# Weight-tile loads moved from SyncE's queue to GpSimd's, and a third buffer for the token blocks

## The chip, the cores and the metric

The kernel runs on all 8 cores of one Trainium2 chip, two cores to a batch element: both compute k and v of all its 4096 tokens, and each the rest for its own 2048 tokens. There is no exchange between cores. The metric is the device time in microseconds of the slowest core.

## The reference

One transformer layer on x of shape (4, 4096, 2048), with sandwich norms:

```python
x = x + layernorm(attn(layernorm(x), Wqkv, Wout))        # 16 heads of 128, RoPE, causal softmax
x = x + layernorm(ffn(layernorm(x), w1, w3, w2))         # hidden size 5461
# ffn: every weight is first made ternary
s = mean(abs(w));  wq = clip(round(w / s), -1, 1) * s
ffn(x) = (silu(x @ w1q.T) * (x @ w3q.T)) @ w2q.T
```

Each of w1, w3 and w2 therefore has to be read twice: once for mean(abs(w)), once to be made ternary.

## The kernel before

The program is written out by hand for five engines, with semaphores. `b.w(engine, sem, value)` is a wait that stands at that place in that engine's instruction stream; `b.dma(queue, ...)` issues a transfer at that place in the stream of SyncE (SP), ScalarE (ACT) or GpSimd (POOL). An engine that waits issues nothing that stands behind the wait. Five phases are divided by barriers.

**Phase 1, projections.** Three parts (q with 16 blocks, k with 32, v with 32) run over blocks of 128 tokens. The 16 MB of float32 weights of a part are loaded as bf16 by eight GpSimd DMAs (`wqkvT`), which wait for TensorE's last instruction of the part before. For block `tb`, `p1_loads(tb+1)` puts the load of the next block (`xin`, 1 MB, two buffers) and its cos and sin rows (`ctile`, `stile`, two buffers) on SP. TensorE makes two halves `dh` of 32 matmuls each (L372, L376). After the first half, `p1_stage_ln(tb+1)` normalizes the next block: VectorE (DVE) sums it (L258), ACT squares it (L260), small operations follow, DVE writes the result (L288), and TensorE transposes it (L299). For q and k, DVE applies RoPE (L390 to L400) to each half, TensorE transposes (L420), DVE copies (L428), and ACT issues four stores. For v, ACT evacuates each half (L407) and issues one store.

At the end of each block comes `emit_spass_tiles(2)`: two tiles of w1, w3 or w2 (139 in all, so they last for the first 70 of the 80 blocks) are loaded on SP into `wtl` (two buffers), ACT takes the absolute sum (L218), and GpSimd adds it to a running sum (L224 for a matrix's first tile, else L228). Before tile k is loaded, SP waits for ACT's sum of tile k-2. GpSimd waits for ACT's sum of tile k before it adds it. Of w1 and w3 every third tile has 1365 columns (682.5 KB), the others have 2048 (1 MB).

**Phase 2, attention.** There are 64 passes: four query slots with 8, 16, 24 and 32 key tiles, and 16 heads in each. In pass p, SP first issues the windows of pass p+2 (q, k and v of that head, `issue_windows`), once TensorE has ended pass p-1. TensorE makes scores (L589), ACT the exponentials (L601), DVE masks the last 8 key tiles (L611), TensorE multiplies with v and with ones (L627, L631); a short tail of the pass before (reciprocal L654, L660, L666, L671) is placed after the second pair. Then comes `emit_quant(3)`: three weight tiles (139 in all, so 46 passes have three and the 47th has one) are loaded on SP into `qtl` (two buffers), DVE makes them ternary in two operations (L523, L528), and ACT issues the store. SP waits for DVE's second operation on tile k-2 before it loads tile k; DVE waits for the load of k and for the store of k-2 (`rstg`, two buffers). As the third tile of a pass uses the buffers of the first, its load is issued when the first is done.

Phases 3 to 5 (output projection, w1 and w3, w2) aren't touched.

Of the kernel before, what the change touches and what calls it, by code (L numbers as in the profile page):

```python
# [48 lines left out]
def bcast_mid(ap2d, rep):  # L49
    return dataclasses.replace(ap2d, ap=[ap2d.ap[0], [0, rep], ap2d.ap[1]])  # L50
# [43 lines left out]
class Bld:  # L94
# [41 lines left out]
    def barrier(self, state):  # L136
        for sem in ["ld", "st"] + [f"d{i}" for i in range(8)] + [f"s{i}" for i in range(4)]:
            self.w("sync", sem, self.cnt[sem])
        for sem in ["sd", "act"] + [f"s{i}" for i in range(4)]:
            self.w("scalar", sem, self.cnt[sem])  # L140
        self.w("gpsimd", "gd", self.cnt["gd"])
        self.w("gpsimd", "gq", self.cnt["gq"])
        self.w("vector", "dve", self.cnt["dve"])
        self.w("tensor", "pe", self.cnt["pe"])
        for e in ENGS:
            inst = self.engobj.nop() if self.eng == e else None
            self.sig(inst, "ph", 1)
        tgt = self.cnt["ph"]
        self.engobj.wait_ge(self.sems["ph"], tgt)
# [3 lines left out]
def emit_program(b, t):  # L153
# [11 lines left out]
    i = b.V.memset(t["ones_f"][:], 1.0)  # L165
# [8 lines left out]
    fa = Carve(FAA, t["FA_COLS"])  # L174
    wsb = bf.take(16 * 2048)
    xnb = [bf.take(2048), bf.take(2048)]
# [2 lines left out]
    qks = [bf.take(1024), bf.take(1024)]  # L179
    fmstg = [bf.take(2048), bf.take(2048)]  # L180
    vstg = [bf.take(2048), bf.take(2048)]
    xin = [fa.take(2048), fa.take(2048)]
    ctile = [fa.take(128), fa.take(128)]
    stile = [fa.take(128), fa.take(128)]
    t1f = [fa.take(1024), fa.take(1024)]
    t2f = [fa.take(1024), fa.take(1024)]
    wtl = [fa.take(2048), fa.take(2048)]
# [14 lines left out]
    sp_done = {}  # L202
    sp_add = {}

    def emit_spass_tiles(n):
        for _ in range(n):
            if sp_idx[0] >= len(sp_tiles):
                return
            k = sp_idx[0]
            mat, r0, f0, fw, acc = sp_tiles[k]  # L210
            rows = 128 if mat != "w2T" else min(128, HID - r0)
            slot = k % 2
            b.w("sync", "act", sp_done.get(k - 2, 0))
            c_ld = b.dma("sync", f"d{4 + slot}", wtl[slot][0:rows, 0:fw],
                         t[mat][r0:r0 + rows, f0:f0 + fw])
            b.w("scalar", f"d{4 + slot}", c_ld)
            b.w("scalar", "gq", sp_add.get(k - 1, 0))
            i = b.A.activation(spscr[0:rows, 0:fw], wtl[slot][0:rows, 0:fw],  # L218
                               AF.Abs, accum_out=stats[0:rows, 28:29])
            c = b.sig(i, "act")  # L220
            sp_done[k] = c
            b.w("gpsimd", "act", c)
            if not acc_init[acc]:
                i = b.G.tensor_scalar(stats[0:rows, acc:acc + 1],  # L224
                                      stats[0:rows, 28:29], 1.0, None, ALU.mult)
                acc_init[acc] = True
            else:
                i = b.G.tensor_add(stats[0:rows, acc:acc + 1],  # L228
                                   stats[0:rows, acc:acc + 1],
                                   stats[0:rows, 28:29])  # L230
            c = b.sig(i, "gq")
            b.w("gpsimd", "gq", c)
            sp_add[k] = c
            sp_idx[0] += 1
# [8 lines left out]
    rope_done = {}  # L243
# [2 lines left out]
    fmstg_free = {}  # L246
    vstg_free = {}
    xin_free = {}
    mm_done = {}
    xnb_cons = {}  # L250
    xhT_mm = {}
# [59 lines left out]
    for pidx, (part, poff, nblk) in enumerate(parts):  # L311
# [13 lines left out]
        cnorm_map = {}  # L325

        def p1_loads(tb):
            par = tb % 2
            dcnt, acnt = xin_free.get(par, (0, 0))
            b.w("sync", "dve", dcnt)  # L330
            b.w("sync", "act", acnt)
            xld_map[tb] = b.dma("sync", f"d{par}", xin[par][:],
                                xsrc_t[tb * 128:(tb + 1) * 128, :])
            if part in ("q", "k"):
                b.w("sync", "dve", rope_done.get((par, 0), 0))
                b.w("sync", "dve", rope_done.get((par, 1), 0))
                b.dma("sync", f"d{2 + par}", ctile[par][:],
                      cos_d[tb * 128:(tb + 1) * 128, :])
                ccs_map[par] = b.dma("sync", f"d{2 + par}", stile[par][:],
                                     sin_d[tb * 128:(tb + 1) * 128, :])  # L340

        def p1_stage_ln(tb):
            par = tb % 2
            b.w("vector", f"d{par}", xld_map[tb])
            b.w("scalar", f"d{par}", xld_map[tb])
            b.w("vector", "pe", xnb_cons.get(par, 0))
            cnorm = ln_normalize(xin[par][:], xnb[par][:], tb)
            xin_free[par] = (cnorm, b.cnt["act"])
            cnorm_map[tb] = cnorm

        def p1_stage_tp(tb):
# [3 lines left out]
            xnb_cons[par] = b.cnt["pe"]  # L355

        p1_loads(0)
        p1_stage_ln(0)
        p1_stage_tp(0)
        for tb in range(nblk):  # L360
            par = tb % 2
            if tb + 1 < nblk:
                p1_loads(tb + 1)
            c_cs = ccs_map.get(par, 0)
            for dh in range(2):
                b.w("tensor", "act", vevac_done.get((dh,), 0))
                b.w("tensor", "dve", rope_done.get(("t1", dh), 0))
                b.w("tensor", "gd", wld)
                b.w("tensor", "dve", xhT_done[par])
                last = None  # L370
                for ec in range(16):
                    i = b.T.matmul(pa[:, dh * 1024: dh * 1024 + 512],  # L372
                                   xhT[par][:, ec * 128:(ec + 1) * 128],
                                   wsb3[:, ec, dh * 1024: dh * 1024 + 512],
                                   start=(ec == 0), stop=(ec == 15))
                    i2 = b.T.matmul(pa[:, dh * 1024 + 512: dh * 1024 + 1024],  # L376
                                    xhT[par][:, ec * 128:(ec + 1) * 128],
                                    wsb3[:, ec, dh * 1024 + 512: dh * 1024 + 1024],
                                    start=(ec == 0), stop=(ec == 15))
                    last = i2 if i2 is not None else i  # L380
                c_mm = b.sig(last, "pe")
                mm_done[(par, dh)] = c_mm
                paH = pa[:, dh * 1024:(dh + 1) * 1024]
                if part in ("q", "k"):
                    b.w("vector", "pe", c_mm)
                    b.w("vector", f"d{2 + par}", c_cs)
                    pa3 = _r(paH, "p (h d) -> p h d", h=8)
                    t13 = _r(t1f[dh][:], "p (h d) -> p h d", h=8)
                    cosb = bcast_mid(ctile[par][:], 8)
                    i = b.V.tensor_tensor(t13, pa3, cosb, ALU.mult)  # L390
                    b.sig(i, "dve")
                    for hf in range(2):
                        ov = half_view(t2f[dh][:], 8, hf)
                        iv = half_view(paH, 8, 1 - hf)
                        sv = half_bcast(stile[par][:], 8, hf)
                        i = b.V.tensor_tensor(ov, iv, sv, ALU.mult)
                        b.sig(i, "dve")
                    b.w("vector", "dve", b.cnt["dve"])
                    b.w("vector", "pe", qks_free.get(dh, 0))
                    i = b.V.tensor_add(qks[dh][:], t1f[dh][:], t2f[dh][:])  # L400
                    c = b.sig(i, "dve")
                    rope_done[("t1", dh)] = c
                    rope_done[(par, dh)] = c
                else:
                    b.w("scalar", "pe", c_mm)
                    b.w("scalar", f"s{2 + par}", vstg_free.get(par, 0))
                    i = b.A.activation(vstg[par][:, dh * 1024:(dh + 1) * 1024],  # L407
                                       paH, AF.Copy)
                    vevac_done[(dh,)] = b.sig(i, "act")
                if dh == 0 and tb + 1 < nblk:  # L410
                    p1_stage_ln(tb + 1)
# [98 lines left out]
    def emit_quant(n):  # L510
        for _ in range(n):
            k = q_idx[0]
            if k >= len(q_tiles):
                return
            mat, rsp, thb, r0, rows, f0, fw = q_tiles[k]
            slot = k % 2
            b.w("sync", "dve", q_v.get(k - 2, 0))
            c_ld = b.dma("sync", f"d{2 + slot}", qtl[slot][0:rows, 0:fw],
                         t[mat][r0:r0 + rows, f0:f0 + fw])
            q_ld[k] = c_ld  # L520
            b.w("vector", f"d{2 + slot}", c_ld)
            b.w("vector", f"s{2 + slot}", q_store.get(k - 2, 0))
            i = b.V.tensor_scalar(sqscr2[slot][0:rows, 0:fw],  # L523
                                  qtl[slot][0:rows, 0:fw],
# [543 lines left out]
def build_program():  # L1068
# [33 lines left out]
    with ExitStack() as ctx:  # L1102
# [10 lines left out]
        t["pa"] = En(nc.psum_tensor("pa", [128, 2048], F32))  # L1113
        t["pb"] = En(nc.psum_tensor("pb", [128, 2048], F32))
        sem_names = (["ld", "gd", "sd", "st", "pe", "dve", "act", "gq", "ph"]
                     + [f"d{i}" for i in range(8)] + [f"s{i}" for i in range(4)])
        sems = {n: En(nc.semaphore(n)) for n in sem_names}
        for val, idx in t["consts"].items():
            nc.const_aps.register(F32, val, t["cpool"][:, idx:idx + 1])
# [116 lines left out]
```

How the kernel before makes its waits and increments, by code:

```python
    def sig(self, inst, sem, n=1):  # L117
        self.cnt[sem] += n
        if inst is not None:
            inst.then_inc(self.sems[sem], n)
        return self.cnt[sem]
# [1 line left out]
    def w(self, eng, sem, val):  # L123
        if val <= 0:
            return
        assert val <= self.cnt[sem], (sem, val, self.cnt[sem])
        if self.eng == eng:
            self.engobj.wait_ge(self.sems[sem], val)
# [7 lines left out]
    def barrier(self, state):  # L136
        for sem in ["ld", "st"] + [f"d{i}" for i in range(8)] + [f"s{i}" for i in range(4)]:
            self.w("sync", sem, self.cnt[sem])
        for sem in ["sd", "act"] + [f"s{i}" for i in range(4)]:
            self.w("scalar", sem, self.cnt[sem])
        self.w("gpsimd", "gd", self.cnt["gd"])
        self.w("gpsimd", "gq", self.cnt["gq"])
        self.w("vector", "dve", self.cnt["dve"])
        self.w("tensor", "pe", self.cnt["pe"])
        for e in ENGS:
            inst = self.engobj.nop() if self.eng == e else None
            self.sig(inst, "ph", 1)
        tgt = self.cnt["ph"]
        self.engobj.wait_ge(self.sems["ph"], tgt)
```

## Time and profile before

| | us |
|---|---|
| median of 2 runs | 7228.25 (6972.67 and 7483.83) |
| the profiled execution | 6924.68 |
| its slowest core, core 3, first to last instruction | 6923.1 |
| the other cores | 6892.8 to 6922.9 |

In the profile of the slowest core TensorE is busy for 70% of the span, DVE for 33%, ACT for 20% and GpSimd for 1%. The chain of work that ended last is 60% TensorE and 17% DVE, and 7% DMA. Busy time is an average over phases that have different limits, so the phases are read one by one. In the rows of idle time, an engine's wait is put down to what ended last before it went on. A DMA's time to landing counts from the start of its issue.

### The profile page before, as it was taken

To read this page: it belongs to the slowest core of one execution; us is meant where nothing else is said; L and a number is where in the kernel's file an instruction comes from. 1 tells how busy PE (TensorE), PEld (TensorE's weight loads), DVE (VectorE), ACT (ScalarE), POOL (GpSimd) and SP (SyncE) were. 2 spreads that over 40 slices of the span, in tenths; PEclk is the share of its full clock that TensorE was granted. 3 is DMA by queue.
4 is the path that set the end of the run, shared out by engine and by line. 5 is a ranking of instruction groups with operands and counts; after the bars stand their busy time and mean duration, and the time that the engine had idled before them with its cause. 6 is when DMAs were issued, how large, how long until landed. Compare 5 with 4: busy or idle time off the path is not lost.

```text
span 6923.1 us, 58985 instructions; the slowest of 8 cores (6892.8 to 6923.1 us)
## 1 busy us (share of the span) xinstructions
PE 4868.7 (70%) x20684; PEld 1976.7 (29%) x20684; DVE 2250.4 (33%) x2417; ACT 1417.6 (20%) x1543; POOL 56.5 (1%) x175
## 2 busy tenths in 40 slices
PE   4775777759964455566579983444999999786666
PEld 2332333324420011111112221222444444332233
DVE  3543555523336655544432222332000000011122
ACT  1221222225411122233345540111000000000000
POOL 0000000000000000000000000000000000000000
PEclk8777888879986677677789986777999999898888
DMA  6446444376445545544533224323222222345544
GB/s 143 125 140 132 130 143 144 125 182 229 168 136 181 196 163 169 181 155 155 170 119 80 69 45 107 91 89 100 64 56 55 55 64 55 101 135 170 172 148 148
DMA packets 763499, 881.28 MB, mean 127 GB/s; under 512 B 538368, under 2 KB 629972, under 8 KB 715302
## 3 DMA queue, kind: packets, MB, share of 16 engines
q1 hardware_dynamic: 552540, 678.95, 31.6%
q10 hardware_dynamic: 177396, 165.01, 7.0%
q0 software_dynamic: 33280, 33.56, 3.4%
q8 instruction: 177, 2.90, 0.2%
q14 instruction: 106, 0.87, 0.1%
HBM read 729.18 MB, written 181.75 MB: 132 GB/s over the span
## 4 chain that ended last, share of the span: by engine, by line
PE 60%; DVE 17%; DMA 7%; issue 7%; ACT 5%; another core or an unknown queue 2%; SPq 1%; ACTq 1%; DVEq 0%; POOL 0%; POOLq 0%
PE pa L882 9%; PE pb L899 9%; PE pa L372 7%; PE pa L376 6%; PE pb L631 5%; PE pb L627 5%; PE pa L985 4%; PE pb L985 4%; PE pa L589 4%; ACT BFA L601 3%; DVE BFA L528 3%; PE pa L749 2%; PE pb L749 2%; PE pb L660 2%; DVE FAA L390 2%
## 5 line engine op out<-in xcount | busy, mean ns | idle before, releaser
L372 PE MATMUL pa<-BFA 128*128 128x512 bf16 x2560 | 1036.9, 405 | 252.1 <-DMA BFA<-wqkvT 174.0
L627 PE MATMUL pb<-BFA 128*128 128x512 bf16 x1280 | 546.7, 427 | 711.9 <-ACT BFA L601 459.8
L376 PE MATMUL pa<-BFA 128*128 128x512 bf16 x2560 | 1033.4, 404 | 0.0
L601 ACT ACTIVATE BFA<-pa,biascsb 128x1024 bf16<-128x1024 f32 x640 | 705.3, 1113 | 1437.6 <-DVE BFA L528 683.2
L882 PE MATMUL pa<-BFA 128*128 128x512 bf16 (+1 forms) x2752 | 603.2, 380 | 37.3 <-DMA BFA<-r3sp 37.3
L899 PE MATMUL pb<-BFA 128*128 128x512 bf16 (+1 forms) x2752 | 601.0, 379 | 0.0
L985 PE MATMUL pa<-BFA 128*128 128x512 bf16 (+1 forms) x1376 | 363.7, 388 | 256.5 <-DMA BFA<-w2rsp 235.9
L631 PE MATMUL pb<-BFA,ones_b 128*1 128x512 bf16 x1280 | 531.3, 415 | 0.0
L909 DVE SCALAR_TENSOR_TENSOR BFA<-pb,stats,BFA 128x2048 bf16<-128x2048 f32 (+1 forms) x43 | 101.1, 2351 | 1128.7 <-PE pb L899 1128.7
L611 DVE TENSOR_TENSOR BFA<-BFA 128x512 bf16<-128x512 bf16 x512 | 195.1, 422 | 834.7 <-ACT BFA L601 834.6
L627 PEld LDWEIGHTS pb<-BFA 128*128 128x128 bf16 x1280 | 127.3, 99 | 1088.3 <-issue 1082.5
L372 PEld LDWEIGHTS pa<-BFA 128*128 128x128 bf16 x2560 | 263.5, 103 | 604.1 <-issue 364.5
L589 PE MATMUL pa<-BFA 128*128 128x512 bf16 x1280 | 420.7, 422 | 20.1 <-DMA BFA<-vsp 20.1
L882 PEld LDWEIGHTS pa<-BFA 128*128 128x128 bf16 (+1 forms) x2752 | 270.7, 98 | 362.7 <-issue 40.5
L899 PEld LDWEIGHTS pb<-BFA 128*128 128x128 bf16 (+1 forms) x2752 | 271.1, 98 | 322.9
L985 PE MATMUL pb<-BFA 128*128 128x512 bf16 (+1 forms) x1376 | 360.3, 385 | 0.0
L376 PEld LDWEIGHTS pa<-BFA 128*128 128x128 bf16 x2560 | 262.4, 102 | 332.2 <-issue 90.3
L218 ACT ACTIVATE BFA<-FAA 128x2048 bf16<-128x2048 f32 (+1 forms) x139 | 247.3, 1779 | 533.1 <-DVE BFA L306 436.3
L528 DVE SCALAR_TENSOR_TENSOR BFA<-FAA,stats 128x2048 bf16<-128x2048 f32 (+1 forms) x139 | 304.2, 2189 | 14.9 <-DVE FAA L523 0.5
L890 ACT ACTIVATE BFA<-pa,stats 128x2048 bf16<-128x2048 f32 (+1 forms) x43 | 84.6, 1967 | 1076.5 <-PE pa L882 1076.5
L390 DVE TENSOR_TENSOR FAA<-pa,FAA 128x1024 f32<-128x1024 f32 x96 | 117.2, 1221 | 572.7 <-PE pa L376 572.7
L420 PE MATMUL pb<-identsb,BFA 128*128 128x128 bf16 x768 | 78.7, 264 | 266.0 <-DVE BFA L400 266.0
(83 smaller groups left out, 3357.0 us busy)
## 6 DMA issues: line engine op xcount, KB each, us to landing
FAA<-w2T SPq DMA_DIRECT2D x84, 1024.0 KB, 7.1
BFA<-w2rsp SPq DMA_DIRECT2D x336, 256.0 KB, 2.8
FAA<-w1T SPq DMA_DIRECT2D x64, 1024.0 KB, 9.0
FAA<-x_tok SPq DMA_DIRECT2D x64, 1024.0 KB, 8.7
FAA<-w3T SPq DMA_DIRECT2D x64, 1024.0 KB, 9.8
BFA<-vsp SPq DMA_DIRECT2D x160, 256.0 KB, 8.0
FAA<-x_own SPq DMA_DIRECT2D x32, 1024.0 KB, 9.0
BFA<-wqkvT POOLq DMA_DIRECT2D x24, 1024.0 KB, 38.4
```

The lines of the kernel that those rows point to most:

```text
L372: i = b.T.matmul(pa[:, dh * 1024: dh * 1024 + 512], xhT[par][:, ec * 128:(ec + 1) * 128], wsb3[:, ec, dh * 1024: dh * 1024 + 512], start=( ...
L376: i2 = b.T.matmul(pa[:, dh * 1024 + 512: dh * 1024 + 1024], xhT[par][:, ec * 128:(ec + 1) * 128], wsb3[:, ec, dh * 1024 + 512: dh * 1024 + ...
L390: i = b.V.tensor_tensor(t13, pa3, cosb, ALU.mult)
L528: i = b.V.scalar_tensor_tensor(rstg[slot][0:rows, 0:fw], qtl[slot][0:rows, 0:fw], stats[0:rows, thb + 1:thb + 2], sqscr2[slot][0:rows, 0:f ...
L589: i = b.T.matmul(pa[:, (2 * pr + kt % 2) * 512:(2 * pr + kt % 2 + 1) * 512], kwin[ring][:, kt * 128:(kt + 1) * 128], qwin[ring][:], start= ...
L601: i = b.A.activation(ptv, pa[:, pr * 1024:(pr + 1) * 1024], AF.Exp, bias=bc2, scale=SCL)
L627: i = b.T.matmul(ovb, vwin[ring][:, kt * 128:(kt + 1) * 128], PTr[ptr][:], start=(kt == 0), stop=(kt == KT - 1))
L631: i = b.T.matmul(lq[0:1, :], t["ones_b"][:], PTr[ptr][:], start=(kt == 0), stop=(kt == KT - 1))
L749: i = b.T.matmul(X[:, o0:o0 + 512], attT[par][:, ec * 128:(ec + 1) * 128], wosb3[:, ec, o0:o0 + 512], start=(ec == 0), stop=(ec == 15))
L882: i = b.T.matmul(pa[0:hw, tq * 512:(tq + 1) * 512], r13[:, ec, :], x2T3[:, ec, tq * 512:(tq + 1) * 512], start=(ec == 0), stop=(ec == 15))
L899: i = b.T.matmul(pb[0:hw, tq * 512:(tq + 1) * 512], r33[:, ec, :], x2T3[:, ec, tq * 512:(tq + 1) * 512], start=(ec == 0), stop=(ec == 15))
L985: i = b.T.matmul(PS[tb][:, f2 * 512:(f2 + 1) * 512], lhs, w2s[ring][0:hw, f2 * 512:(f2 + 1) * 512], start=(hc == 0), stop=(hc == NHC - 1))
```

## The change

In `emit_spass_tiles` and in `emit_quant` the weight-tile loads are issued by GpSimd in place of SP, with semaphores of their own (g0 to g3), and the waits for their buffers move with them. In phase 1, `xin`, `ctile` and `stile` get a third buffer, and `p1_loads` is called two blocks ahead. The condition on which the cos and sin rows are loaded follows the three buffers. The barrier waits for the new semaphores on GpSimd.

```diff
-            b.w("sync", "act", sp_done.get(k - 2, 0))
-            c_ld = b.dma("sync", f"d{4 + slot}", wtl[slot][0:rows, 0:fw],
+            b.w("gpsimd", "act", sp_done.get(k - 2, 0))
+            c_ld = b.dma("gpsimd", f"g{slot}", wtl[slot][0:rows, 0:fw],
                          t[mat][r0:r0 + rows, f0:f0 + fw])
-            b.w("scalar", f"d{4 + slot}", c_ld)
+            b.w("scalar", f"g{slot}", c_ld)
             b.w("scalar", "gq", sp_add.get(k - 1, 0))
```

```diff
         def p1_loads(tb):
-            par = tb % 2
-            dcnt, acnt = xin_free.get(par, (0, 0))
+            sl3 = tb % 3
+            xsem = ("d0", "d1", "d6")[sl3]
+            csem = ("d2", "d3", "d7")[sl3]
+            dcnt, acnt = xin_free.get(sl3, (0, 0))
             b.w("sync", "dve", dcnt)
             b.w("sync", "act", acnt)
...
-                b.w("sync", "dve", rope_done.get((par, 0), 0))
-                b.w("sync", "dve", rope_done.get((par, 1), 0))
+                b.w("sync", "dve", cs_lastuse.get(tb % 3, 0))
...
         p1_loads(0)
+        p1_loads(1)
         p1_stage_ln(0)
...
-            if tb + 1 < nblk:
-                p1_loads(tb + 1)
+            if tb + 2 < nblk:
+                p1_loads(tb + 2)
```

```diff
-            b.w("sync", "dve", q_v.get(k - 2, 0))
-            c_ld = b.dma("sync", f"d{2 + slot}", qtl[slot][0:rows, 0:fw],
+            b.w("gpsimd", "dve", q_v.get(k - 2, 0))
+            c_ld = b.dma("gpsimd", f"g{2 + slot}", qtl[slot][0:rows, 0:fw],
                          t[mat][r0:r0 + rows, f0:f0 + fw])
             q_ld[k] = c_ld
-            b.w("vector", f"d{2 + slot}", c_ld)
+            b.w("vector", f"g{2 + slot}", c_ld)
             b.w("vector", f"s{2 + slot}", q_store.get(k - 2, 0))
```

## Rows read from the trace of the kernel before

**Rows 1.** Busy time by stretch, core 3: q, k, v with tiles, v without, attention

```profile
core 3: us, PE busy (x) PEld busy (x) DVE busy (x) ACT busy (x) POOL busy (x), PEclk, DMA share, GB/s
575.00:1413.00 838.00, 605.87 (x3060) 303.17 (x3061) 445.16 (x542) 187.27 (x254) 16.50 (x69) 0.82 0.42 135
1469.00:1822.00 353.00, 328.73 (x1760) 158.04 (x1760) 115.08 (x153) 179.54 (x216) 7.98 (x42) 0.99 0.58 216
1822.00:1980.00 158.00, 147.47 (x784) 70.73 (x784) 48.72 (x64) 42.26 (x58) 0.19 (x1) 1.00 0.24 85
2000.00:3570.00 1570.00, 870.37 (x2328) 204.80 (x2328) 818.58 (x792) 409.43 (x372) 0.00 (x0) 0.71 0.51 170
```

**Rows 2.** Waits of the engines, whole span: us, times, longest

```profile
ACT BFA L601 <- DVE BFA L528: 683.2, 47, 16.8
PE pb L627 <- ACT BFA L601: 459.8, 56, 15.4
PE pa L372 <- DMA BFA<-wqkvT: 174.0, 3, 60.0
```

**Rows 3.** Timeline of one block of k: ACT, then DVE

```profile
808.53 1.91 ACT L218 ACTIVATE BFA<-FAA 128x2048 bf16<-128x2048 f32 x1 [9.70 <-DVE BFA L306]
814.72 0.18 ACT L260 ACTIVATION_READ_ACCUMULATOR BFA<-FAA 128x1 f32 x1
...
822.40 2.28 DVE L258 TENSOR_REDUCE stats<-FAA 128x1 f32<-128x2048 f32 x1
824.86 0.15 DVE L265 TENSOR_SCALAR stats<-stats 128x1 f32<-128x1 f32 x1 [0.17 <-DVE stats L258]
...
835.86 1.34 ACT L218 ACTIVATE BFA<-FAA 128x1365 bf16<-128x1365 f32 x1 [9.68 <-DVE BFA L306]
```

**Rows 4.** Timeline of one block of v: ACT, then GpSimd

```profile
1534.67 1.91 ACT L218 ACTIVATE BFA<-FAA 128x2048 bf16<-128x2048 f32 x1 [0.56 <-ACT BFA L407]
1537.09 1.91 ACT L218 ACTIVATE BFA<-FAA 128x2048 bf16<-128x2048 f32 x1 [0.42 <-POOL stats L228]
1542.14 1.02 ACT L407 ACTIVATE BFA<-pa 128x1024 bf16<-128x1024 f32 x1 [3.04 <-PE pa L376]
1550.63 1.91 ACT L218 ACTIVATE BFA<-FAA 128x2048 bf16<-128x2048 f32 x1 [0.56 <-ACT BFA L407]
...
1536.81 0.19 POOL L228 TENSOR_TENSOR stats<-stats 128x1 f32<-128x1 f32 x1 [13.35 <-ACT BFA L218]
```

**Rows 5.** Timeline of GpSimd at the end of part k

```profile
1407.55 0.19 POOL L228 TENSOR_TENSOR stats<-stats 128x1 f32<-128x1 f32 x1 [1.67 <-ACT BFA L218]
1408.65 7.74 POOL L133 DMA_DIRECT2D BFA<-wqkvT  x8 [0.92 <-POOL stats L228]
```

**Rows 6.** One load alone: SP's x_tok in late v, then GpSimd's last wqkvT of part k

```profile
L133 SPq DMA_DIRECT2D FAA<-x_tok x6: 327/328/328, 1851.8 to 1931.6; - x6
DMA to landing us min/median/max: 5.2/5.2/5.4
...
L133 POOL DMA_DIRECT2D BFA<-wqkvT x1: 887/887/887, 566.6 to 566.6; - x1
DMA to landing us min/median/max: 8.9/8.9/8.9
```

**Rows 7.** Timeline of DVE, ACT's queue and SP at the end of an attention pass

```profile
2564.52 2.35 DVE L528 SCALAR_TENSOR_TENSOR BFA<-FAA,stats 128x2048 bf16<-128x2048 f32 x1
2566.79 1.28 DVE L523 TENSOR_SCALAR FAA<-FAA,stats 128x2048 f32<-128x2048 f32 x1
2567.36 0.38 SPq L133 DMA_DIRECT2D BFA<-qsp  x1
2573.28 0.93 DVE L523 TENSOR_SCALAR FAA<-FAA,stats 128x1365 f32<-128x1365 f32 x1 [2.75 <-DMA r3sp<-BFA]
2576.55 2.12 ACT L601 ACTIVATE BFA<-pa,biascsb 128x1024 bf16<-128x1024 f32 x2 [14.19 <-DVE BFA L528]
```

**Rows 8.** Landing there: the third tile's load, the first's store, v windows

```profile
L133 SPq DMA_DIRECT2D FAA<-w3T x1: 327/327/327, 2566.9 to 2566.9; - x1
DMA to landing us min/median/max: 6.1/6.1/6.1
...
L133 ACTq DMA_DIRECT2D r3sp<-BFA x1: 361/361/361, 2566.9 to 2566.9; - x1
DMA to landing us min/median/max: 6.2/6.2/6.2
...
DMA to landing us min/median/max: 9.1/9.2/9.2
```

**Rows 9.** DVE's L523 over all of attention: what its idle time ended with

```profile
  DMA w2rsp<-BFA: 50.4, 14
  DMA r3sp<-BFA: 43.7, 16
  DMA r1sp<-BFA: 42.4, 16
```

More of the change, by code:

```diff
@@ L140, in barrier @@
             self.w("scalar", sem, self.cnt[sem])
-        self.w("gpsimd", "gd", self.cnt["gd"])
-        self.w("gpsimd", "gq", self.cnt["gq"])
+        for sem in ["gd", "gq"] + [f"g{i}" for i in range(4)]:
+            self.w("gpsimd", sem, self.cnt[sem])
         self.w("vector", "dve", self.cnt["dve"])
@@ L181, in emit_program @@
     vstg = [bf.take(2048), bf.take(2048)]
-    xin = [fa.take(2048), fa.take(2048)]
-    ctile = [fa.take(128), fa.take(128)]
-    stile = [fa.take(128), fa.take(128)]
+    xin = [fa.take(2048), fa.take(2048), fa.take(2048)]
+    ctile = [fa.take(128), fa.take(128), fa.take(128)]
+    stile = [fa.take(128), fa.take(128), fa.take(128)]
     t1f = [fa.take(1024), fa.take(1024)]
@@ L248, in emit_program @@
     xin_free = {}
+    cs_lastuse = {}
     mm_done = {}
@@ L327, in p1_loads @@
         def p1_loads(tb):
-            par = tb % 2
-            dcnt, acnt = xin_free.get(par, (0, 0))
+            sl3 = tb % 3
+            xsem = ("d0", "d1", "d6")[sl3]
+            csem = ("d2", "d3", "d7")[sl3]
+            dcnt, acnt = xin_free.get(sl3, (0, 0))
             b.w("sync", "dve", dcnt)
             b.w("sync", "act", acnt)
-            xld_map[tb] = b.dma("sync", f"d{par}", xin[par][:],
+            xld_map[tb] = b.dma("sync", xsem, xin[sl3][:],
                                 xsrc_t[tb * 128:(tb + 1) * 128, :])
             if part in ("q", "k"):
-                b.w("sync", "dve", rope_done.get((par, 0), 0))
-                b.w("sync", "dve", rope_done.get((par, 1), 0))
-                b.dma("sync", f"d{2 + par}", ctile[par][:],
+                b.w("sync", "dve", cs_lastuse.get(tb % 3, 0))
+                b.dma("sync", csem, ctile[sl3][:],
                       cos_d[tb * 128:(tb + 1) * 128, :])
-                ccs_map[par] = b.dma("sync", f"d{2 + par}", stile[par][:],
+                ccs_map[sl3] = b.dma("sync", csem, stile[sl3][:],
                                      sin_d[tb * 128:(tb + 1) * 128, :])
@@ L343, in p1_stage_ln @@
             par = tb % 2
-            b.w("vector", f"d{par}", xld_map[tb])
-            b.w("scalar", f"d{par}", xld_map[tb])
+            sl3 = tb % 3
+            xsem = ("d0", "d1", "d6")[sl3]
+            b.w("vector", xsem, xld_map[tb])
+            b.w("scalar", xsem, xld_map[tb])
             b.w("vector", "pe", xnb_cons.get(par, 0))
-            cnorm = ln_normalize(xin[par][:], xnb[par][:], tb)
-            xin_free[par] = (cnorm, b.cnt["act"])
+            cnorm = ln_normalize(xin[sl3][:], xnb[par][:], tb)
+            xin_free[sl3] = (cnorm, b.cnt["act"])
             cnorm_map[tb] = cnorm
@@ L361, in emit_program @@
             par = tb % 2
-            if tb + 1 < nblk:
-                p1_loads(tb + 1)
-            c_cs = ccs_map.get(par, 0)
+            sl3 = tb % 3
+            if tb + 2 < nblk:
+                p1_loads(tb + 2)
+            c_cs = ccs_map.get(sl3, 0)
             for dh in range(2):
@@ L385, in emit_program @@
                     b.w("vector", "pe", c_mm)
-                    b.w("vector", f"d{2 + par}", c_cs)
+                    b.w("vector", ("d2", "d3", "d7")[sl3], c_cs)
                     pa3 = _r(paH, "p (h d) -> p h d", h=8)
                     t13 = _r(t1f[dh][:], "p (h d) -> p h d", h=8)
-                    cosb = bcast_mid(ctile[par][:], 8)
+                    cosb = bcast_mid(ctile[sl3][:], 8)
                     i = b.V.tensor_tensor(t13, pa3, cosb, ALU.mult)
@@ L394, in emit_program @@
                         iv = half_view(paH, 8, 1 - hf)
-                        sv = half_bcast(stile[par][:], 8, hf)
+                        sv = half_bcast(stile[sl3][:], 8, hf)
                         i = b.V.tensor_tensor(ov, iv, sv, ALU.mult)
@@ L403, in emit_program @@
                     rope_done[(par, dh)] = c
+                    cs_lastuse[sl3] = c
                 else:
@@ L1115, in build_program @@
         sem_names = (["ld", "gd", "sd", "st", "pe", "dve", "act", "gq", "ph"]
-                     + [f"d{i}" for i in range(8)] + [f"s{i}" for i in range(4)])
+                     + [f"d{i}" for i in range(8)] + [f"s{i}" for i in range(4)]
+                     + [f"g{i}" for i in range(4)])
         sems = {n: En(nc.semaphore(n)) for n in sem_names}
```

## The prediction

> **What bounds the kernel now.** I read the busy time by stretch first, because the page's 70% for TensorE hides several limits [rows 1]. In parts q and k TensorE is busy for 606 of 838 us and waits each block for DVE. In v it is busy for 329 of 353 us at a granted clock of 0.99, so that part is TensorE's. In the attention stretch, up to 3570 us, it is busy for 870 of 1570 us. The list of waits says why [rows 2]: ACT's exponentials wait 683 us, 47 times, for DVE's L528, that is for the weight tiles made ternary between two passes, and TensorE waits 460 us for those exponentials. At the start of the three parts TensorE waits 174 us for weights.
>
> What the change could free is therefore looked for in waits for transfers that SP issues late. There are next to none: the list has no wait for x_tok, cos or sin in steady state, and none for an attention window but one of 20 us. SP's own long waits cost nothing, since what stands behind them arrives before it is wanted. So the third buffers and the earlier block loads remove no wait, and I cost them at nothing; they are hidden behind a block's matmuls, 16 us in v and 27 us in k.
>
> **Phase 1: the order on GpSimd.** This is the step that matters. SP today has two tile loads in flight. On GpSimd the load of tile k+1 stands behind two waits that were harmless there: "ACT's sum of tile k is done" and "my add of tile k is done". The condition written for the load is still k-2, but the stream reads: load k, wait for ACT(k), add k, load k+1. The two loads of a block can't overlap any more, and no tile load is in flight while ACT sums.
>
> The loop for one tile is: from ACT's start to the end of the add, 1536.81 + 0.19 - 1534.67 = 2.33 us [rows 4]; from the end of an add to the start of a DMA on GpSimd, 0.92 us [rows 5]; the landing L; about 0.1 us for ACT to start. That is L + 3.35 us per tile. No row shows a 1 MB float32 tile from this queue. Below, SP's block load of 1 MB lands alone in 5.2 us with an issue of 0.33 us; GpSimd's issue takes 0.89 us, so 5.2 + 0.56 = 5.8. Above, GpSimd's last weight load of 1 MB, which comes in shorter runs, lands in 8.9 us [rows 6]. I take L = 7.0, nearer the block load, which has the same long rows, plus something because one of the two tile loads will meet a block load.
>
> The Trainium skill, "DMA: Bandwidth & Descriptors", section "Latency and other measured facts", gives about 1 us to the first byte on the software path against about 0.6 us on the hardware one. By that the lower bound would be 5.6 and the sum about 9 us less at that end; no row here separates it.
>
> *v.* A block takes 15.96 us today, from 1534.67 to 1550.63 [rows 4]. Two tiles take 2 x (7.0 + 3.35) = 20.7 us. ACT's other work (two evacuations, the square and two small operations) fits into the second load, and TensorE with its 15.96 us of work runs ahead, so the tile loop becomes the bound: +4.74 us a block. Tiles 96 to 138 fall on v, 43 tiles or 21.5 blocks: **+102 us**. With L = 5.8 the block takes 18.3 us and the sum is +50; with L = 8.9 it is 24.5 us and +184. Only with L under 4.6 would it cost nothing.
>
> *q and k.* There is cover. With ACT's first sum starting at t = 0 (808.53), DVE wants the square of the next block when its own reduction ends, at 824.68, t = 16.15 [rows 3]; today the square ends at 814.90. Afterwards: second load starts at 3.25, lands at 3.25 + L, second sum 2.1 us, square 2.1 us with gaps, ready at L + 7.6. With L = 7 that is 14.6, inside the cover; with 8.9 it is 0.35 us late, in the two thirds of 48 blocks whose second tile is a large one, 11 us in all. The other condition, both loops within one block of 27.3 us, holds up to L = 10.3. **0**, range 0 to 11.
>
> *Starts of k and v.* GpSimd issues the new weights only after its last add, and the second tile of the last block is later by L + 0.9 = 8 us, twice: +16. Against it, SP's first two tile loads (2 MB) no longer share the start with the weights, of which 16 MB take about 57 us, while one more block load (1 MB) does: 1 MB less, 3.5 us, three times: -10. **+6**, range -11 to +20.
>
> **Phase 2.** GpSimd has nothing else here, so the order is sound. The first two tiles of a pass are loaded long before use, as now. The third can't be: its buffer comes free with the first tile's L528, at 2566.87. Today SP issues it at 2566.9, it lands 6.1 us later (2573.0), and the store of the first tile, which must also be out, lands at 2573.15; DVE goes on at 2573.28 [rows 7, 8]. The profile names the store in all 46 waits, 136.5 us [rows 9], but the load is 0.15 us behind it. DVE's third tile, ACT's stores in its queue and then the exponentials follow, so a later landing is paid in full. The terms: the longer issue, +0.56; the start of a DMA on GpSimd after a wait, half of the 0.92 us seen in rows 5, +0.45; and the windows of pass p+3. These stand behind this load on SP today (first at 2567.36), and will go ahead of it as soon as TensorE has ended the pass, some 2 us earlier, on another queue: their v parts land in 9.2 us [rows 8], and I count +0.85 for sharing. Less 0.15 of slack, that is 1.7 us for each of 46 passes: **+78 us**. Below: only the longer issue counts, 0.4 us, +18. Above: it lands as slowly as the v windows do, 9.2 + 0.9 against 6.1, 4.0 us, +184.
>
> **Sum** against the profiled execution: 6924.7 + 102 + 0 + 6 + 78 = 7111 us. The faster of the two other runs is 48 us above that execution, the median of the two, 7228, is far above both; I put the forecast between the profiled execution and the faster run, 24 us up: **7135 us**, 2.7% slower than before.
>
> **Rivals.**
> 1. *The loads are quick enough (within 2%).* L = 5.8 and 0.4 us a pass: +50 in v, +3 at the starts (2 x 6.7 - 10), +18 in attention: +71, 6996 us. For it: one load in flight lands faster than two, as the 5.2 us show. Against it: even then both loops lose. Chance 0.22.
> 2. *Descriptor writing on GpSimd is held up by DVE.* The third tile's load is released exactly when DVE starts L523 on the second tile, 1.28 us [rows 7]. If GpSimd can't proceed in that time, each of 46 passes pays 1.28 us more, +59: 7194 us. For it: the placing is exact. Against it: no row of attention has a GpSimd DMA. The Trainium skill, "SBUF — State Buffer", section "SBUF: two separate sides", states such a lock against GpSimd while a copy-like DVE operation runs in a two-port mode. By that rule this rival holds; the trace can't say, though L523's 2048 columns in 1.28 us against L528's in 2.35 us are the pace of such a mode. Chance 0.25.
> 3. *Faster.* The wait before the third tile is ended by the load and not by the store, and a queue of its own, free of SP's windows, brings it at once. All of the 136.5 us could go [rows 9]; against +108 in phase 1 the total would be 28 us under, 6897; with L = 5.8 it is 6842. It decides only if the load lands 2 us earlier and the store too, but its release doesn't move, and today nothing stands ahead of it on SP. Chance 0.05.
>
> **How the numbers follow.** The forecast has 0.48, and the three rivals 0.22, 0.25 and 0.05. The two slower cases hold 0.73. The range begins at rival 1 with the lower end of the starts (-11 in place of +3), 6982, rounded to 6985, and ends where both upper bounds meet: 6925 + 184 + 11 + 20 + 184 = 7324, and 48 for the distance between runs: 6985 to 7370. Slower by over 2% (about what this kernel's measurement tells from no change) needs +138: forecast and rival 2, 0.73. Within 2%: 0.22. Faster: 0.05.
>
> **What would show it.** In the profile after, ACT's L218 should wait for a DMA from w2T in v, and a v block should take 20 to 21 us with TensorE's share falling from 93% to about 72%; GpSimd's loads should stand 10 us apart, never two in flight. A k block should stay at 27.3 us. In attention the wait before every third L523 should grow from 3 to 4.7 us and be put down to the load. The forecast is wrong if v keeps its 16 us (then L is under 4.6), if k blocks grow (then L is over 8.5), or if the third tile's wait doesn't grow.

## The result, and the profile after

The changed kernel is slower: its time is 1.0276 times the time before, with a 95% interval of 1.0198 to 1.0354, which begins just under 1.02. The medians of all runs are 7286.85 us (11 runs, 7138.74 to 7589.81) and 7156.83 us (10 runs, 6929.78 to 7483.83). Both hold executions in which the cores of a die ran at a lower granted clock, and the ratio is over those without. The profiled execution took 7180.79 us, against 6924.68 before.

The stages, each as the median over the eight cores of the profiled execution with the lowest and highest core behind it, are read from the first and last start of the lines that open and close them:

| stage, us | before | after | difference |
|---|---|---|---|
| start to last RoPE transpose (q, k) | 1388 (1371 to 1402) | 1395 (1379 to 1417) | +7 |
| from there to the last projection matmul (v) | 580 (579 to 582) | 647 (639 to 654) | +67 |
| from there to the first scores | 25 (23 to 26) | 30 (26 to 33) | +5 |
| attention with ternary tiles | 1548 (1539 to 1552) | 1672 (1656 to 1680) | +124 |
| attention without them, to the output projection | 637 (630 to 642) | 638 (634 to 640) | +1 |
| output projection | 615 | 616 | 0 |
| w1 and w3 | 1238 | 1238 | 0 |
| w2 (start of first to start of last matmul) | 820 (814 to 824) | 823 (819 to 886) | +4 |

The stages that the change doesn't touch agree, but for two cores: in w2 cores 6 and 7 need 883 and 886 us where the others need about 820, with matmuls of 417 ns on core 7 in place of 388. Without these 63 us core 7 (7179.3 us) wouldn't be the slowest; core 5 (7144.5 us) would, so some 35 us of the 256 us between the two profiled executions come from there and not from the change. The profile is read below on core 3, which had nothing of it (7097.5 us; core 3 is also the core shown of before).

In part v, ACT, then GpSimd, core 3 after, one block and the beginning of the next (start, length, what, idle time before it and what ended that):

```profile
1540.08 1.91 ACT L218 ACTIVATE BFA<-FAA 128x2048 bf16<-128x2048 f32 x1 [0.56 <-ACT BFA L414]
1550.11 1.91 ACT L218 ACTIVATE BFA<-FAA 128x2048 bf16<-128x2048 f32 x1 [8.02 <-DMA FAA<-w2T]
1558.84 1.91 ACT L218 ACTIVATE BFA<-FAA 128x2048 bf16<-128x2048 f32 x1 [1.53 <-DMA FAA<-w2T]
...
1542.24 0.18 POOL L228 TENSOR_TENSOR stats<-stats 128x1 f32<-128x1 f32 x1 [8.93 <-ACT BFA L218]
1543.04 0.57 POOL L133 DMA_DIRECT2D FAA<-w2T  x1 [0.62 <-POOL stats L228]
1552.26 0.18 POOL L228 TENSOR_TENSOR stats<-stats 128x1 f32<-128x1 f32 x1 [8.66 <-ACT BFA L218]
1553.06 0.57 POOL L133 DMA_DIRECT2D FAA<-w2T  x1 [0.62 <-ACT BFA L414]
```

The second sum, which waited 0.42 us for an add in [rows 4], now waits 8.02 us for its load. The load begins 0.62 us after the add of the tile before it: never two in flight. The block takes 18.8 us where it took 15.96, and 19.0 us on average over the 17 blocks from 1465 to 1789 us.

The order on GpSimd isn't all that sets the block's length. In 8 blocks ACT's first sum waits for ACT's own evacuation and not for its load, as here:

```profile
1787.44 1.02 ACT L414 ACTIVATE BFA<-pa 128x1024 bf16<-128x1024 f32 x1 [2.56 <-PE pa L382]
1789.03 1.91 ACT L218 ACTIVATE BFA<-FAA 128x2048 bf16<-128x2048 f32 x1 [0.56 <-ACT BFA L414]
...
1779.54 0.57 POOL L133 DMA_DIRECT2D FAA<-w2T  x1 [0.62 <-POOL stats L228]
```

This load landed 6.1 us after 1779.54, more than 3 us before the sum began; ACT stood waiting for TensorE, whose granted clock is 0.81 in this block. Over 1469 to 1869 us the granted clock is 0.91 (0.99 in [rows 1]) and TensorE is busy for 85% of the time.

At the end of an attention pass, DVE, GpSimd and SP, core 3 after:

```profile
2647.12 2.35 DVE L535 SCALAR_TENSOR_TENSOR BFA<-FAA,stats 128x2048 bf16<-128x2048 f32 x1
2649.39 1.28 DVE L530 TENSOR_SCALAR FAA<-FAA,stats 128x2048 f32<-128x2048 f32 x1
2657.98 0.93 DVE L530 TENSOR_SCALAR FAA<-FAA,stats 128x1365 f32<-128x1365 f32 x1 [4.85 <-DMA FAA<-w3T]
...
2650.03 0.75 POOL L133 DMA_DIRECT2D FAA<-w3T  x1 [22.54 <-DVE BFA L535]
2653.68 0.53 POOL L133 DMA_DIRECT2D FAA<-w3T  x1 [2.89 <-DVE BFA L535]
...
2647.02 0.33 SPq L133 DMA_DIRECT2D BFA<-qsp  x1
2647.87 1.05 SPq L133 DMA_DIRECT2D BFA<-vsp  x2
```

Before, the third tile went on 6.4 us after the first tile's release, and the store was named [rows 7, 8]; now it goes on 2657.98 - 2649.47 = 8.5 us after it, and the load is named. SP's windows start 3 us ahead of the tile's load, where they stood behind it. Over all 46 passes DVE's idle time before L530, 136.5 us in [rows 9], is now

```profile
  DMA FAA<-w2T: 95.8, 14
  DMA FAA<-w3T: 83.0, 16
  DMA FAA<-w1T: 74.0, 16
```

252.8 us in all: +116, close to the +124 of the stage. That is 5.5 us a pass in place of 3.0.

### The profile page after: what moved, and what is told of

It is laid out like the page before. It is cut to its first block, busy times and chain, and to the rows that moved or that the text cites. A ratio compares the mean times of both kernels' runs of the same rounds, so it can differ in the third digit from the quotient of the medians.

```text
span 7179.3 us, 58949 instructions; the slowest of 8 cores (7097.5 to 7179.3 us)
## 1 busy us (share of the span) xinstructions
PE 4954.8 (69%) x20684; PEld 1995.3 (28%) x20684; DVE 2251.2 (31%) x2417; ACT 1415.3 (20%) x1543; POOL 222.1 (3%) x453
## 4 chain that ended last, share of the span: by engine, by line
PE 57%; DVE 16%; DMA 10%; issue 6%; ACT 6%; another core or an unknown queue 2%; SPq 1%; ACTq 1%; DVEq 0%; POOL 0%; POOLq 0%
PE pa L889 8%; PE pb L906 8%; PE pa L378 5%; PE pa L992 5%; PE pa L382 5%; PE pb L992 5%; PE pb L638 5%; PE pb L634 4%; PE pa L596 4%; DMA FAA<-w2T 3%; ACT BFA L608 3%; DVE BFA L535 3%; DMA FAA<-w1T 2%; DMA FAA<-w3T 2%
## 5 line engine op out<-in xcount | busy, mean ns | idle before, releaser
L889 PE MATMUL pa<-BFA 128*128 128x512 bf16 (+1 forms) x2752 | 603.3, 380 | 37.1 <-DMA BFA<-r3sp 37.1
L906 PE MATMUL pb<-BFA 128*128 128x512 bf16 (+1 forms) x2752 | 601.0, 379 | 0.0
L992 PE MATMUL pa<-BFA 128*128 128x512 bf16 (+1 forms) x1376 | 397.6, 416 | 257.9 <-DMA BFA<-w2rsp 237.2
L992 PE MATMUL pb<-BFA 128*128 128x512 bf16 (+1 forms) x1376 | 393.8, 413 | 0.0
```

The lines of the kernel that those rows point to most:

```text
L889: i = b.T.matmul(pa[0:hw, tq * 512:(tq + 1) * 512], r13[:, ec, :], x2T3[:, ec, tq * 512:(tq + 1) * 512], start=(ec == 0), stop=(ec == 15))
L906: i = b.T.matmul(pb[0:hw, tq * 512:(tq + 1) * 512], r33[:, ec, :], x2T3[:, ec, tq * 512:(tq + 1) * 512], start=(ec == 0), stop=(ec == 15))
L992: i = b.T.matmul(PS[tb][:, f2 * 512:(f2 + 1) * 512], lhs, w2s[ring][0:hw, f2 * 512:(f2 + 1) * 512], start=(hc == 0), stop=(hc == NHC - 1))
```

## The experiments

The theory under test is that of the prediction: v is longer because GpSimd's stream takes the second load out of flight, and attention is longer because every third tile lands later. The rivals are the third buffers, GpSimd's queue being slow in itself, descriptor writing held up by DVE, and the windows that now share the DMA engines. Stage times are medians over the cores, as above.

**One part alone, first.** The diff of each is the part of the change that its name says.

```diff
# e1_sums_only: before, with
-            b.w("sync", "act", sp_done.get(k - 2, 0))
-            c_ld = b.dma("sync", f"d{4 + slot}", wtl[slot][0:rows, 0:fw],
+            b.w("gpsimd", "act", sp_done.get(k - 2, 0))
+            c_ld = b.dma("gpsimd", f"g{slot}", wtl[slot][0:rows, 0:fw],
# e2_ternary_only: before, with
-            c_ld = b.dma("sync", f"d{2 + slot}", qtl[slot][0:rows, 0:fw],
+            c_ld = b.dma("gpsimd", f"g{2 + slot}", qtl[slot][0:rows, 0:fw],
# e3_buffers_only: the changed kernel with both of these back on SP
```

> Only the tile loads of the absolute sums (phase 1) go to GpSimd's queue; the ternary tiles and the two block buffers stay as before. If the order of GpSimd's stream (load, wait for ACT, add, load) costs the time of phase 1, part v takes about 647 us as after the change, against 580 before (median of the cores, from the last RoPE transpose to the last projection matmul), and the attention stretch with ternary tiles keeps its 1548 us: in all about +75 us, 1.01 times before. If the third buffers are what costs or saves in v, it stays at 580.

> Only the loads of the ternary tiles (attention) go to GpSimd's queue. If the later landing of every third tile explains the attention, its stretch from the first to the last ternary tile takes about 1672 us, +124, and v stays at 580: about 1.018 times before. If part of the 124 us came from what phase 1 leaves behind, it is less.

> Only the third buffers for block, cos and sin and the loads two blocks ahead; all tile loads stay on SP. The theory that no block load was ever late says 1.00 times before, with q and k at about 1388 us and v at 580. A rival, that the earlier loads disturb others (the weights at the start of a part or ACT's tiles), says q and k grow by the 7 us that the changed kernel shows, or more.

| | q, k | v | attention with ternary tiles | ratio to before |
|---|---|---|---|---|
| e1_sums_only | 1439 | 664 (least: 643) | 1549 | none |
| e2_ternary_only | 1393 | 580 | 1670 | 1.0164 (1.0138 to 1.0190) |
| e3_buffers_only | 1402 | 582 | 1549 | none |

The two parts add up to the change and don't touch each other's stage: v is long only with the sum tiles on GpSimd, attention only with the ternary tiles on it. The profile of e1 is of an execution at a granted clock of 0.78 to 0.80, so its least core (643 us in v) is the one to set beside the 639 to 654 of the changed kernel. The third buffers change neither stage. Whether they, or anything else, add the 7 us of q and k can't be told: 1386 to 1402 us were measured there for e2, e3 and e4, and single cores of before spread over 31 us.

**The order on GpSimd mended.** In the changed kernel, the next tile's load goes ahead of the wait for ACT.

```diff
+        sp_load(k)
+        sp_load(k + 1)     # wait for ACT(k-1), load k+1 on GpSimd; each tile once
...
-            b.w("gpsimd", "act", sp_done.get(k - 2, 0))
-            c_ld = b.dma("gpsimd", f"g{slot}", wtl[slot][0:rows, 0:fw], ...)
```

> The changed kernel, but GpSimd issues the load of tile k+1 ahead of its wait for ACT's sum of tile k, so that two loads are in flight as on SP before. If the order alone made v longer, v is back at 580 us while attention keeps 1672: about 67 us less than the changed kernel, 1.019 times before. If loads through GpSimd's queue are slower in themselves (longer landing, held up descriptor writing), v stays above 600.

Part v takes 579 us, attention 1672 us, and the ratio to before is 1.0158 (1.0120 to 1.0197). In v, core 3, ACT and GpSimd:

```profile
1499.72 1.91 ACT L229 ACTIVATE BFA<-FAA 128x2048 bf16<-128x2048 f32 x1 [0.56 <-ACT BFA L425]
1502.15 1.91 ACT L229 ACTIVATE BFA<-FAA 128x2048 bf16<-128x2048 f32 x1 [0.43 <-POOL stats L239]
1515.68 1.91 ACT L229 ACTIVATE BFA<-FAA 128x2048 bf16<-128x2048 f32 x1 [0.56 <-ACT BFA L425]
...
1502.67 0.57 POOL L133 DMA_DIRECT2D FAA<-w2T  x1 [0.62 <-POOL stats L239]
1505.10 0.57 POOL L133 DMA_DIRECT2D FAA<-w2T  x1 [0.62 <-POOL stats L239]
```

The two loads are 2.4 us apart, ACT waits for neither, and the block is back at 15.96 us. The granted clock over 1460 to 1800 us is back at 1.00. The queue is the same and the loads are the same: the whole +67 us comes from the order of GpSimd's stream, TensorE's lower clock in v included.

**Windows held back.** Two places at which SP may go on to the windows of pass p+3, in the changed kernel.

```diff
         b.w("sync", "pe", win_free.get(p - 3, 0))
...
+        b.w("sync", "dve", q_v.get(3 * (p - 3), 0))        # e6: first tile of pass p - 3 is done
...
+        b.w("sync", f"g{2 + k3 % 2}", q_ld[k3])            # e10: its third tile (k3) has landed
```

> The changed kernel, but SP holds back the windows of pass p+3 until DVE has finished the first ternary tile of pass p, the moment at which SP reached them before the change. If the windows that go ahead on another queue are what makes the third tile land 1.7 us later (7.8 against 6.1), its wait falls by 1 to 1.7 us a pass and the stretch from 1672 to about 1600 us. If the longer way of a GpSimd DMA is the whole cause, it stays at about 1672 us.

> The changed kernel, but SP holds back the windows of pass p+3 until the third ternary tile of pass p has landed. If the windows sharing the DMA engines make that load slow, it lands about as fast as the same queue's loads in phase 1 (5.4 to 5.7 us for 1 MB) or the load on SP before (6.1 us), the wait before the third tile falls from about 5 to 3 us and the stretch with ternary tiles from 1672 to about 1590 us. If a transfer from GpSimd's queue is slow there for another reason, landing stays at 7.8 us and the stretch at 1672 us, or grows where windows are now late.

With e6 SP reaches the windows when the tile's load is released, as before the change, but on another queue. The third tile's load of the pass at 2681 us landed in 8.7 us, no better than the 7.8 us above. The stretch took 1707 us at a granted clock of 0.79, which can't be set beside 1672; but DVE's idle time before L530, which is a wait for the load, is 274 us in all where it was 253. The expected gain didn't come. With e10 the stretch is **1557 us** against 1672. Core 3, DVE, GpSimd and SP at the end of a pass:

```profile
2652.47 2.35 DVE L535 SCALAR_TENSOR_TENSOR BFA<-FAA,stats 128x2048 bf16<-128x2048 f32 x1
2657.90 0.93 DVE L530 TENSOR_SCALAR FAA<-FAA,stats 128x1365 f32<-128x1365 f32 x1 [3.08 <-DMA FAA<-w3T]
...
2651.73 0.75 POOL L133 DMA_DIRECT2D FAA<-w3T  x1 [23.15 <-DVE BFA L535]
...
2657.80 0.33 SPq L133 DMA_DIRECT2D BFA<-qsp  x1
```

The load that landed 7.8 us after its issue lands in 6.0, and DVE waits 3.08 us. The landing of the small tiles over 2560 to 3000 us (count, size, median to landing), after, then e10:

```profile
FAA<-w3T POOLq DMA_DIRECT2D x13, 682.5 KB, 7.9
```

```profile
FAA<-w3T POOLq DMA_DIRECT2D x13, 682.5 KB, 5.6
```

DVE's idle time before L530 falls to 141.7 us, against 136.5 us before. So 115 of the 124 us in attention are there only while the windows are in flight ahead of the load. What remains, 9 us or 0.2 us a pass, is less than the spread of the cores (1548 to 1573 us), and is the most that GpSimd's longer way to a DMA costs.

The packets show what the load waits for. The first two rows are the changed kernel from the start of the third tile's issue to its first packet (2650.03 to 2654.3 us), the third is e10 over the same piece of the pass above (2651.73 to 2653.8 us). q1 is SP's queue, q10 ACT's, q0 GpSimd's:

```profile
q1 hardware_dynamic: 2168, 0.82, 83.5%
q10 hardware_dynamic: 91, 0.37, 23.1%
```

```profile
q10 hardware_dynamic: 140, 0.52, 64.0%
```

In the changed kernel 2168 packets of SP's queue move in these 4.3 us and none of the tile's. In five passes from 2650 to 2790 us the tile's first packet comes 3.7 to 4.3 us after the start of its issue, and in five passes of e10 1.8 to 2.1 us after it. It fits e6 too: the two are released at one moment, but SP's and ACT's packets come first, from 2681.5 us on, and the tile's first packet some 4.4 us after the start of its issue. In SP's one queue, before the change, the tile stood ahead of the windows.

The Trainium skill, "DMA: Bandwidth & Descriptors", section "Queues, rings and completion order", says that each DMA engine takes turns between the queues that have work for it, and consumes one queue in order. Turns show before the change between the tile's load on SP's queue and the first tile's store on ACT's (82 and 85 packets from 2569.5 to 2571.5 us). Between the windows and the tile on GpSimd's queue the trace shows none for these 4.3 us, though e10 has the first packet after 2. Why, no run here shows.

**Does DVE hold up GpSimd's descriptor writing?** Filler operations on spare memory, in the changed kernel, put ahead of the second tile, where the third tile's load is released.

```diff
+            if k % 3 == 1:   # e7: one source, 4096 columns
+                i = b.V.tensor_scalar(spare[:], spare[:], 1.0, None, ALU.mult)
+                                # e8: two sources, 2048 columns, in its place
+                i = b.V.scalar_tensor_tensor(spare[:, 0:2048], spare[:, 0:2048], 1.0,
+                                             spare[:, 2048:4096], ALU.mult, ALU.add)
```

> The changed kernel with an extra DVE operation that computes nothing of use: 4096 float32 columns of spare memory times 1.0 (one source, about 2.56 us at the rate of L530), put ahead of the second ternary tile of each pass, exactly where the third tile's load is released. DVE waits 4.9 us for that load anyway. If DVE's operation holds up GpSimd's descriptor writing, the load is issued only when the filler ends, about 1.3 us later than now, and the stretch grows by 46 x 1.3 = 60 us or more. If not, the filler disappears in the wait and the stretch stays at 1672 us.

> The control for the run before: the same place, but a filler with two sources over 2048 columns, 2.35 us at the rate of L535. Both theories expect the GpSimd issue to be quick and the filler to disappear in the wait: about 1672 us. If this one grows too, time on DVE itself is what counts and the other run shows no lock.

Core 3, the filler and GpSimd's issue, e7 and then e8:

```profile
2663.03 2.29 DVE L529 TENSOR_SCALAR FAA<-FAA 128x4096 f32<-128x4096 f32 x1
...
2663.68 1.76 POOL L133 DMA_DIRECT2D FAA<-w3T  x1 [22.86 <-DVE BFA L539]
```

```profile
2664.32 2.28 DVE L529 SCALAR_TENSOR_TENSOR FAA<-FAA 128x2048 f32<-128x2048 f32 x1
...
2664.97 0.53 POOL L133 DMA_DIRECT2D FAA<-w3T  x1 [22.62 <-DVE BFA L540]
```

The lock is there. Under the one-source filler the issue takes 1.76 us and ends at 2665.44, 0.12 us after the filler's end at 2665.32; under the two-source filler it takes 0.53 us and ends while the filler still runs. The Trainium skill, "SBUF — State Buffer", section "SBUF: two separate sides", states this lock, and in "A bandwidth-pool intuition that's wrong (but worth ruling out)" about 115 ns from DVE's end; the traces agree with both. But it isn't what the change costs: in the changed kernel L530 lasts 1.28 us and GpSimd starts 0.64 us into it, so the issue takes 0.75 us in place of 0.53, at most 0.22 us a pass. And the expected growth of 60 us in e7 didn't come: the stretches take 1660 and 1659 us. The issue held up for 1.23 us cost e7 nothing against e8, because the load doesn't move sooner without it: in three passes each, from 2697 to 2771 us, the tile's first packet comes 3.5 to 3.8 us after the start of the issue in e7 and 3.7 to 4.8 us after it in e8. The windows hold it up longer than the lock does. That both stretches are 12 us shorter than the changed kernel's is left unexplained; the cores of the three overlap (1651 to 1669, 1640 to 1667 and 1656 to 1680 us).

**Three buffers for the ternary tiles.** In the kernel before (e5, run again as e5_again), and in the changed kernel together with the mended order (e9).

```diff
-    rstg = [bf.take(2048), bf.take(2048)]
-    qtl = [fa.take(2048), fa.take(2048)]
+    rstg = [bf.take(2048) for _ in range(3)]
+    qtl = [fa.take(2048) for _ in range(3)]
...
-            b.w("sync", "dve", q_v.get(k - 2, 0))
+            b.w("sync", "dve", q_v.get(k - 3, 0))
```

> The kernel before (all loads on SP), with three buffers in place of two for the loaded and the finished ternary tiles. Every third tile then waits neither for a load issued 6 us earlier nor for a store. If that wait (136.5 us in all before) is on the path that sets the end, the attention stretch falls from 1548 to about 1412 us and the kernel to 0.980 times before. If it was covered by something else (ACT, the store queue), it falls by less.

> The kernel before with three buffers for the ternary tiles once more, for a ratio: its ternary stretch took 1417 us against 1548 before. That wait was on the path, so 131 us less of 6925: 0.981 times before. A rival, that the saved time comes back as a lower granted clock elsewhere, says 0.99 or more.

> The changed kernel with both of its losses mended: the load of the next sum tile ahead of the wait for ACT, and three buffers for ternary tiles, all tile loads still on GpSimd's queue. If the queue itself is harmless where a load is issued early enough, part v takes 579 us and the ternary stretch 1417 us, as with SP. If the queue costs something in itself, the stretch stays above 1430 us.

The stretch takes 1417 us in e5 and 1416 us in e5_again, 131 us under before, and the ratio of e5_again is 0.9839 (0.9753 to 0.9925). The interval doesn't shut out the 0.99 of its rival; the profile speaks against it, with 6789 us in place of 6925 and no core at a lower granted clock than before (0.838 and more, against 0.827 and more). DVE's three tiles stand shoulder to shoulder there (core 3):

```profile
2518.76 1.28 DVE L524 TENSOR_SCALAR FAA<-FAA,stats 128x2048 f32<-128x2048 f32 x1
2520.14 2.35 DVE L529 SCALAR_TENSOR_TENSOR BFA<-FAA,stats 128x2048 bf16<-128x2048 f32 x1
2522.41 0.93 DVE L524 TENSOR_SCALAR FAA<-FAA,stats 128x1365 f32<-128x1365 f32 x1
```

With all tile loads on GpSimd, e9 has 579 us in v (one core 673) and 1416 us in the stretch: the queue is harmless where a load is issued early enough. Of e9 there is one profile and no ratio.

**A version that beats both.** From e5: no ternary tile in the first 16 passes, three in each pass after them, behind the tail of the pass before, and the stores on GpSimd. No run separates these three edits.

```diff
                 prev_tail[0]()
                 prev_tail[0] = None
+            if ktp == 2 and p >= 16:
+                emit_quant(3)
...
-        emit_quant(3)
...
-            q_store[k] = b.dma("scalar", ("s2", "s3", "st")[r3],
+            q_store[k] = b.dma("gpsimd", ("g0", "g1", "g2")[r3],
```

> The kernel before with three buffers for ternary tiles, but no ternary tile in the first 16 passes (8 key tiles), three in each of the 47 passes from the 17th on, placed behind the tail of the pass before, where DVE has no mask to apply, and the stores on GpSimd's queue in place of ACT's. ACT's exponentials then wait for no ternary tile. Today that wait is 683 us in all. If it is all on the path and DVE's 10 us a pass fit beside the pairs without a mask (8 to 24 key tiles, 8 to 26 us), the attention shortens by 450 to 600 us and the kernel to 0.91 to 0.94 times before. If DVE's work only moves (passes of 16 key tiles leave 8.5 us without masks for 10 us of ternary work), the gain is 250 to 400 us.

Its time is **0.9538 times before (0.9510 to 0.9565)**. From the first scores to the output projection it takes 1882 us, against 2197 before and 2067 in e5_again: -315, so the lower of the two expectations held. ACT's wait for the ternary operation, 683 us in [rows 2], has left the list, and TensorE's wait for the exponentials has shrunk to 109 us, but TensorE now waits for DVE's masks (core 3, us, times, longest):

```profile
PE pb L628 <- DVE BFA L612: 307.1, 148, 11.9
PE pb L628 <- ACT BFA L602: 109.4, 81, 1.6
```

The masks of a pass stand behind 10 us of ternary work on DVE (core 3, one pass, and then DVE's idle time before L524 over all 46):

```profile
2909.20 1.29 DVE L524 TENSOR_SCALAR FAA<-FAA,stats 128x2048 f32<-128x2048 f32 x1 [7.27 <-DMA FAA<-w3T]
2917.54 1.64 DVE L529 SCALAR_TENSOR_TENSOR BFA<-FAA,stats 128x1365 bf16<-128x1365 f32 x1
2919.10 1.42 DVE L612 TENSOR_TENSOR BFA<-BFA 128x512 bf16<-128x512 bf16 x4
...
2901.55 2.78 SPq L133 DMA_DIRECT2D FAA<-w3T  x3
...
  DMA FAA<-w3T: 107.0, 16
  DMA FAA<-w2T: 105.4, 14
  DMA FAA<-w1T: 70.5, 16
```

That work is one limit, and it begins late: DVE first waits 7.27 us for the pass's first tile, 283 us in 46 passes, because SP issues the tiles at 2901.55, behind the windows (from 2895.34), which wait for TensorE. It is the theme of this document once more, a load that stands behind another's wait in one stream. No run here mends it.

## Why the prediction was right or wrong

**What bounds the kernel, and the third buffers.** Right: no block load was late, and e3 leaves v at 582 and attention at 1549 us.

**Phase 1, v.** The mechanism was right, and e1 and e4 show it from both sides. Its size, +102 us, was too large; it measured +67, 3.1 us a block in place of 4.74. Two terms of the loop were mis-sized, and one was missing. The start of a DMA comes 0.62 us after an add, not 0.92 as in [rows 5]; the trace of before has 0.61 too, at the start of part k (510.55 us). And L = 7.0 is near one of the two loads only: the first of a pair lands in 6.6 us on average and the second in 5.6, 6.1 over the 42 loads of v. With these the loop would be 2 x (6.1 + 3.05) = 18.3 us, an estimate, where 19.0 was measured. The rest goes with what was put at nothing: TensorE was taken to run ahead, and ACT's evacuation to fit in. In 8 blocks it didn't; TensorE's granted clock in the part was 0.91, and its share fell to 85%, not to 72%.

**q and k.** Predicted 0, measured +7, inside the spread of the cores. The cover held: the second sum waits there 6.6 us for its load, and DVE waits 1.9 us in all for the square behind it, in two of 29 blocks.

**Starts of k and v.** Predicted +6, and the sign was wrong: TensorE's waits for the weights, in all, are 4 to 16 us shorter on each core (158.4 us on core 3, where [rows 2] has 174.0).

**Phase 2.** The direction and the place were right (every third tile, its load now named), the size was not: 1.7 us a pass and +78 us were predicted, 2.7 us and +124 us measured. Inside that sum two terms were wrong in opposite ways. The way through GpSimd was put at 0.56 + 0.45 us; it costs 0.2 us. The windows' sharing was put at 0.85 us; e10 shows 115 us, 2.5 us a pass. I had counted them as early by some 2 us and as sharing with the load; they are 3 us ahead of it, and the load's first packet moves only when theirs are nearly through.

**The sum and the stated time.** The sum over the profiled execution was +186 us, 2.7% slower, and 1.0276 was measured. That is partly luck: v was put 35 us too high, attention 46 us too low. The stated time, 7135 us, was wrong. It lies below both medians of before, 7228.25 and 7156.83 us, so as a statement on medians it reads as a gain, and 152 us below the 7286.85 us of after. The step that failed is the last one: with two runs of before 511 us apart, I tied the time to the profiled execution and went up by 24 us, to a place where neither kernel's median lies. A forecast that is set beside a median has to start from it, and to put the sum on as a ratio: 7228 x 1.027 = 7423 us by the median that was known, 7157 x 1.027 = 7350 us by that of ten runs. Neither would have been exact, but both have the sign that the sum had. The stated range, 6985 to 7370, holds the median.

**The rivals.** Rival 1 (within 2%) fell by its terms, since both loops lost more than +50 and +18 us, and just about by the time, whose interval begins at 1.0198. Rival 2 had a real mechanism and the wrong price, at most 0.22 us a pass and not 1.28, since GpSimd reaches its issue when half of that operation is over and waits only for the rest. Rival 3 fell: the load landed later, not earlier.

## What to carry to other kernels

In a hand-written stream the wait in front of an instruction is not its condition: everything ahead of it on that engine is. A load moved to an engine that also consumes the result loses its prefetch, unless it is issued ahead of that engine's own waits. And moving a transfer to a queue of its own takes away the order that one queue gave: ask what now runs beside it, and give an urgent load a buffer, so that it can be issued early, before giving it a queue.

## What was not expected of the hardware

- Two queues at once cost the urgent load more than anything in the issuing engine: 7.9 us against 5.6 us for 682.5 KB (medians of 13), from 1152 KB of windows in the other queue. The first packet comes 3.7 to 4.3 us after the start of the issue in place of 1.8 to 2.1.
- The quicker of v's two 1 MB loads from GpSimd's queue is nearly as quick as one from SP's: 5.8 us to ACT's start against 5.2 us to landing in [rows 6]. The issue takes 0.57 us, not the 0.89 us of the weights' DMAs.
- The lock between DVE's one-source operation and GpSimd's DMA issue: 1.76 us in place of 0.53, ending 0.12 us after DVE, and none under a two-source operation (0.53 us). Even so the load landed no later: its first packet was held up longer by the windows.
